# The attention stage's diagonal term and head maximum: added behind the turned sums, and spread by one product with repeated weights

## The chip, the cores and the metric

The kernel runs on one core of a Trainium2 chip, as one launch. The metric is the time of one execution on the device in microseconds (us), the median over several runs. The engines are TensorE (PE in the profile, its loads of stationary operands PEld), VectorE (DVE), ScalarE (ACT), GpSimd (POOL) and SyncE (SP).

## What is computed

A vision tower over 16 images of 512 tokens, width 192: Fourier features and a projection, attention with an optimal-transport plan in place of the usual scores, a layer norm, a mixture of eight experts (two per token), and a layer norm. The change lies in the attention alone. Cut to it (12 heads of width 16):

```python
def _sot(q):                                   # per image and head, N = 512
    qn = q / (norm(q, axis=-1) + 1e-08)
    C = where(eye, 1000.0, 1.0 - einsum('bhnd,bhmd->bhnm', qn, qn))
    log_K = -C / 0.1
    log_v = 0
    for _ in range(10):
        log_u = log_marg - logsumexp(log_K + log_v[..., None, :], axis=-1)
        log_v = log_marg - logsumexp(log_K + log_u[..., :, None], axis=-2)
    z = exp(log_u[..., :, None] + log_K + log_v[..., None, :])
    z = z / max(z, axis=(-2, -1))              # the head's own maximum
    return where(eye, 1.0, z)
attn = softmax(_sot(q) * 16 ** -0.5, axis=-1)
out = einsum('bhnm,bhmd->bhnd', attn, v)
```

## The kernel before, in words

Four stages follow one another: `embed` (features and first projection), `project` (q and v), `attend`, and `mix` with `combine` (experts and norms). Only `attend` is touched.

`attend` works on 48 groups of 4 heads (3 groups per image). The kernel matrix K of a head (512 x 512, four blocks of 128 rows, as high and low f16 part) is built once, and the 20 half iterations are products of K with a vector x, then a reciprocal. Three groups are in flight at any time. Phase G does four things side by side: it builds K of group G+1 (`build`), runs the first half iterations of group G (`young`), the later ones of group G-1 (`old`), and finishes group G-2 (`fin`, its last steps in phase G+1: `tail`). A phase has 10 cycles, `i = 5 * f + c`; f = 0 serves heads a = 0 and b = 1 of the group, f = 1 heads a = 2 and b = 3. The text calls a cycle c0 to c4 of either half. Phases 3 to 44 run in a hardware loop with one image (three phases) per turn; the others are written out.

In each cycle TensorE does `multiply(0)` and `multiply(1)`, each 64 narrow products (12 columns of weights, placed in one of four column strips of the array, L643). ScalarE copies the result out (`read_rows`, L771), TensorE turns it with two f32 products against constant weights each (`turn`, L653), and VectorE makes the next x from it with three small operations (`split`, L885 to L889), for which the next `multiply` waits.

What finishes a head h:

- `u_to_rows` (L677) brings u into rows; VectorE forms the plan z (`join` L908, `times_u` L920) and, block by block, the maximum of each row, and then of each partition (`head_max`, L925).
- Over the partitions the maximum goes by two products and two VectorE operations. `max_to_row` (L683) turns the column `head_max` into one row in PSUM; `largest` (L929) takes the maximum of this row on one partition (`all_max`, 1 x 1); `spread_max` (L687) multiplies it with a row of 4.0 on one partition (`fours`), so that every partition has 4 times the maximum; `scale_of` (L933) takes the reciprocal (`p_scale`). L683 stands in c2 (head a) and c4 (head b), behind the two `multiply` and ahead of `turn(0)`; L687 in the same cycle, ahead of `turn(1)`.
- ScalarE turns z into exp(z * p_scale - 0.25) (`weights`, L794).
- `times_v` (L697) multiplies with v: 16 f32 products of 17 columns of weights (16 of v and a one, for the row sum). Behind them stand 4 more (L700), which add v times the constant diagonal `lift` = 1 - exp(-0.25) for the tokens' own term. `times_v` stands in c4 (head a) and in c1 of the following half (head b).
- ScalarE copies the sums out (`read_v`, L798); `turn_v` (L707) turns them back with one f32 product of 128 columns of weights into `trp`; VectorE divides (`normalise`, L943, L947). `turn_v` stands in c0 and in c3.

Every engine works through its list strictly in the order in which it is written; semaphores join them (`after(engine, semaphore, count)` waits).

Of the kernel before, what the change touches and what calls it, by code (L numbers as in the profile page):

```python
# [488 lines left out]
def attend(nc, q_parts, v_parts, ident, pick_rows, att):  # L489
# [6 lines left out]
    with ExitStack() as ctx:  # L496
# [4 lines left out]
        def sem(name):  # L501
# [13 lines left out]
        fours = sb("fours", [1, P], F32)  # L515
# [12 lines left out]
        all_max = sb("all_max", [1, 1], F32)  # L528
# [13 lines left out]
        max_row, max_all = u_rows[0:1, 0:P], u_rows[:, P:P + 1]  # L542
# [13 lines left out]
        max_row_ready, all_max_ready, max_spread, scale_ready, p_ready = (  # L556
            sem("max_row_ready"), sem("all_max_ready"), sem("max_spread"), sem("scale_ready"), sem("p_ready"))
# [26 lines left out]
        def _(sp):  # L584
# [20 lines left out]
            def phase(G, t, s, young=False, old=False, build=False, fin=False, tail=False):  # L605
# [5 lines left out]
                if old:  # L611
                    after(sp, pv_ready, (G - 3) * GH)
                    load_v(t - 1 if s == 0 else t, (s + 2) % 3)
# [10 lines left out]
        def _(pe):  # L624
# [56 lines left out]
            def max_to_row(F, h):  # L681
                after(pe, head_max_ready, F * GH + h + 1)
                nc.tensor.matmul(max_row, head_max[:, :], eye[:, :], start=True, stop=True).then_inc(max_row_ready, 1)  # L683

            def spread_max(F, h):
                after(pe, all_max_ready, F * GH + h + 1)
                nc.tensor.matmul(max_all, fours[:, :], all_max[:, :], start=True, stop=True).then_inc(max_spread, 1)  # L687

            def times_v(F, s, h, image):
# [5 lines left out]
                for j in range(TB):  # L695
                    for c in range(TB):
                        nc.tensor.matmul(pv[32 * c:32 * c + HD + 1, 0:P], v_sb[s][:, j, h, :], plan[h % 2][:, j, c * P:(c + 1) * P],  # L697
                                         start=(j == 0), stop=False)
                for c in range(TB):
                    last = nc.tensor.matmul(pv[32 * c:32 * c + HD + 1, 0:P], v_sb[s][:, c, h, :], lift[:, :],  # L700
                                            start=False, stop=True)
                last.then_inc(pv_ready, 1)

            def turn_v(F, h):
                H = F * GH + h
                after(pe, pv_read, H + 1)
                nc.tensor.matmul(trp_flat, pv_sb[:, :], to_chunks, start=True, stop=True).then_inc(pv_turned, 1)  # L707

            def phase(G, t, s, young=False, old=False, build=False, fin=False, tail=False):
                mine, before, new = s, (s + 2) % 3, (s + 1) % 3  # L710
                t_fin, t_new = (t if s == 2 else t - 1), (t + 1 if s == 2 else t)
                for i in range(CYCLES):
# [13 lines left out]
                    if c == 2 and fin:  # L726
                        max_to_row(G - 2, a)
                    if c == 4 and fin:
                        max_to_row(G - 2, b)
# [4 lines left out]
                    if c == 0 and f == 0 and tail:  # L734
                        turn_v(G - 3, GH - 2)
                    if c == 0 and f == 1 and fin:
                        turn_v(G - 2, a - 2)
# [8 lines left out]
                    if c == 2 and fin:  # L746
                        spread_max(G - 2, a)
                    if c == 4 and fin:
# [1217 lines left out]
```

## Time and profile before

| | |
|---|---|
| time, median of 3 runs | 5770.17 us (5761.57 to 5798.24) |
| the profiled execution, its own time | 5812.22 us |
| its span in the trace | 5810.4 us |
| PE busy | 4788.6 us (82%) |
| DVE busy | 4015.8 us (69%) |
| ACT busy | 3119.7 us (54%) |
| POOL busy | 840.2 us (14%) |
| attention stage, from about 1582 to 4577 us | 2995 us; PE busy 2842.0, DVE 2146.6, ACT 1712.9 |

The profiled execution is one run, 42 us above the median of the runs. "Busy" of TensorE counts the modelled durations of single products, which overlap; how long it really takes for something is read from the starts of consecutive rows of the timeline.

### The profile page before, as it was taken

The page shows a single profiled execution, that of the slowest core. Times are in us where ns is not written, and L with a number is a line of the kernel's source. Part 1 is how long each engine was busy: PE and PEld are TensorE (multiplying, and loading weights), DVE is VectorE, ACT ScalarE, POOL GpSimd, SP SyncE. Part 2 cuts the span into 40 slices and gives each one's busy share as a digit, 9 for nine tenths or more (in the row PEclk, how much of TensorE's full clock was granted, in tenths as well). Part 3 has the DMA queues.
Part 4 walks back from the last instruction along what each step waited for, and adds up shares of the span by engine and source line. Part 5 has one row for each costly group of instructions (what it writes and reads, how often), then busy time and mean ns, then how long its engine had stood idle before and what let it go on. Part 6 is the DMA issues. An engine that isn't in the chain of part 4 may idle for free. (4 is left out here: it accounts for less than half of the span.)

```text
span 5810.4 us, 201644 instructions
## 1 busy us (share of the span) xinstructions
PE 4788.6 (82%) x86322; PEld 3667.1 (63%) x86323; DVE 4015.8 (69%) x8485; ACT 3119.7 (54%) x4426; POOL 840.2 (14%) x394
## 2 busy tenths in 40 slices
PE   4766776677679999999999999999999289699950
PEld 2444554454358888888888888887888245477740
DVE  8888888985537777777777777777777634355545
ACT  4665666664356556655556555565564223277740
POOL 2444444442000000000000000000000013400026
PEclk9888988888889999999999999999999656699985
DMA  1000000001310000000000000000000212222223
GB/s 55 24 24 24 13 24 24 24 13 42 101 26 15 15 20 15 17 18 15 20 15 19 16 15 20 15 19 16 15 16 7 83 54 75 88 64 69 68 64 98
DMA packets 186937, 198.44 MB, mean 34 GB/s; under 512 B 86848, under 2 KB 167040, under 8 KB 183552
## 3 DMA queue, kind: packets, MB, share of 16 engines
q1 hardware_dynamic: 173824, 160.79, 9.2%
q0 software_dynamic: 12288, 25.18, 1.4%
q8 instruction: 697, 11.42, 0.8%
q14 instruction: 128, 1.05, 0.1%
HBM read 123.00 MB, written 62.91 MB: 32 GB/s over the span
## 5 line engine op out<-in xcount | busy, mean ns | idle before, releaser
L643 PE MATMUL y_ps<-k_sb,x_sb 128*12 128x256 f16 x58368 | 1718.4, 276 | 30.1 <-issue 14.1
L643 PEld LDWEIGHTS y_ps<-k_sb,x_sb 128*12 128x12 bf16 x58368 | 1438.2, 89 | 227.9 <-issue 48.8
L257 PE MATMUL acc<-w_hl,feat_h 128*128 128x384 f16 x3456 | 645.1, 351 | 425.3 <-DVE h_sb L203 297.8
L771 ACT ACTIVATE y_sb<-y_ps 128x256 f32<-128x256 f32 x912 | 348.9, 383 | 1031.9 <-PE y_ps L643 1031.9
L257 PEld LDWEIGHTS acc<-w_hl,feat_h 128*128 128x128 f16 x3456 | 356.9, 104 | 688.7 <-issue 372.9
L150 POOL TENSOR_TENSOR feat_l<-work,feat_h 128x2048 f16<-128x2048 f32 x96 | 576.7, 6008 | 777.6 <-ACT feat_h L241 739.1
L780 ACT ACTIVATE k_new<-cos,k_bias 128x512 f32<-128x512 f32 x768 | 520.4, 682 | 162.9 <-PE cos L670 162.9
L653 PEld LDWEIGHTS turned_x<-rows_in,y_sb 128*128 128x128 f32 x3648 | 477.2, 191 | 138.4 <-issue 93.3
L653 PE MATMUL turned_x<-rows_in,y_sb 128*128 128x16 f32 x3648 | 552.5, 265 | 9.5 <-ACT y_sb L771 9.2
L920 DVE CUSTOM_DVE_ANT_0 plan<-plan,u_rows,v_last 128x512 f32<-128x512 f32 x768 | 535.3, 744 | 4.1
L885 DVE RECIPROCAL x_sb<-turned_x 128x16 f32<-128x16 f32 x864 | 223.6, 259 | 433.2 <-PE turned_x L653 433.1
L241 ACT ACTIVATE feat_h<-work 128x4096 f16<-128x4096 f32 x96 | 388.2, 4044 | 200.2 <-PE acc L264 198.2
L794 ACT ACTIVATE plan<-plan,p_bias,p_scale 128x1024 f32<-128x1024 f32 x384 | 464.3, 1238 | 11.8 <-DVE p_scale L933 11.8
L908 DVE TENSOR_TENSOR plan<-k_sb 128x1024 f32<-128x1024 f16 x384 | 459.8, 1218 | 0.0
L937 DVE TENSOR_TENSOR k_sb<-k_new,k_sb 128x2048 f16<-128x2048 f32 x192 | 436.7, 2274 | 30.1 <-ACT k_sb L788 30.1
L1112 POOL PARTITION_ALL_REDUCE all_maxes<-maxes x1 | 0.4, 374 | 3014.4 <-DVE maxes L1131 3014.4
L194 DVE TENSOR_TENSOR feat_l<-work,feat_h 128x2048 f16<-128x2048 f32 x96 | 320.2, 3335 | 155.5 <-ACT feat_h L241 155.5
L177 DVE TENSOR_SCALAR work<-xt,fr 128x2048 int32<-128x2048 f32 x144 | 387.9, 2720 | 0.0
L788 ACT ACTIVATE k_sb<-k_new 128x2048 f16<-128x2048 f32 x192 | 366.6, 1909 | 10.0
L235 ACT ACTIVATE work<-work 128x2048 f32<-128x2048 f32 x96 | 203.4, 2119 | 311.9 <-DVE work L186 309.6
L264 PE MATMUL acc<-w_hl,feat_l 128*128 128x192 f16 x3456 | 306.4, 248 | 34.2 <-DVE feat_l L194 31.0
L668 PE MATMUL cos<-q_right,q_left 128*128 128x512 f16 x768 | 259.5, 391 | 81.9 <-issue 37.9
(255 smaller groups left out, 7427.1 us busy)
## 6 DMA issues: line engine op xcount, KB each, us to landing
xt<-in_x_dram SPq DMA_DIRECT2D x16, 1280.0 KB, 5.8
x_in_sb<-expert_rows SPq DMA_DIRECT2D x39, 384.0 KB, 3.2
expert_results<-y_sb SPq DMA_DIRECT2D x39, 384.0 KB, 2.5
q_left<-q_parts SPq DMA_DIRECT2D x192, 64.0 KB, 2.9
q_right<-q_parts SPq DMA_DIRECT2D x192, 64.0 KB, 3.0
v_parts<-v_sb SPq DMA_DIRECT2D x16, 408.0 KB, 2.4
v_in_sb<-v_parts SPq DMA_DIRECT2D x48, 136.0 KB, 3.4
h_tokens<-h_sb SPq DMA_DIRECT2D x16, 384.0 KB, 2.5
```

The source lines that it names most:

```text
L150: nc.gpsimd.tensor_tensor(feat_l[n][:, 1, 0:hi], waves[n][:, 1, 0:hi], feat_h[n][:, 1, 0:hi], ALU.subtract).then_inc(low_cos_ready[n], 1)
L177: last = nc.vector.tensor_scalar(whole[:, lo:hi], xt[a][:, lo:hi], fr[:, f:f + 1], None, ALU.mult)
L241: nc.scalar.activation(feat_h[n][:, :, 0:hi], waves[n][:, :, 0:hi], ACT.Copy).then_inc(high_ready[n], 1)
L257: nc.tensor.matmul(acc[a][:, q, 0:2 * DIM], block_of, w_hl[:, k, :, :].rearrange("p a d -> p (a d)"), start=(k == 0), stop=False)
L643: last = nc.tensor.matmul(y[a][32 * c:32 * c + XW, :, :], high[:, j, XW * h:XW * (h + 1)], k_sb[s][:, h, :, at:at + P], start=(h == 0 and ...
L653: last = nc.tensor.matmul(tr_flat[a], y_sb[a][:, part, :], add_parts, start=(part == 0), stop=(part == 1))
L780: nc.scalar.activation(k_new[h % 2][:, c, :], cos[:, c % 2, :], ACT.Exp, bias=k_bias[:, 0:1], scale=1.0 / (REG * Q_SCALE ** 2), accum_out= ...
L788: nc.scalar.activation(k_sb[s][:, h, 0, :], k_new[h % 2][:, :, :].rearrange("p b n -> p (b n)"), ACT.Copy).then_inc(k_high, 1)
L794: nc.scalar.activation(part, part, ACT.Exp, bias=p_bias[:, 0:1], scale=p_scale[h % 2][:, 0:1]).then_inc(p_ready, 1)
L908: done = nc.vector.tensor_tensor(plan[h % 2][:, 2 * half:2 * half + 2, :].rearrange("p b n -> p (b n)"), k_sb[s][:, h, 0, cols], k_sb[s][: ...
L920: last = nc.vector.tensor_tensor_reduce(plan[h % 2][:, c, :], plan[h % 2][:, c, :], u_rows[:, :], v_last[s][:, c, h:h + 1], 0.0, ALU.mult, ...
L937: nc.vector.tensor_tensor(k_sb[s][:, h, 1, :], k_new[h % 2][:, :, :].rearrange("p b n -> p (b n)"), k_sb[s][:, h, 0, :], ALU.subtract).the ...
```

## The change

Two steps of the finish of a head are computed otherwise.

The diagonal: the four narrow f32 products at the end of `times_v` are gone. Instead `turn_v` first multiplies v, as the moving operand with 68 columns, by the diagonal `lift`, with 128 columns of weights, into `trp`, and the product that turns the sums is added to it.

The maximum: `max_to_row`, `largest` and `spread_max` are gone. `max_to_rows` uses the column `head_max`, repeated 128 times, as weights and a diagonal of 4.0 (`eye_four`) as moving operand, so that every partition gets the whole row of maxima (times 4). `scale_of` takes the maximum of its partition's row and then the reciprocal; both stand on VectorE ahead of `next_x(0)`. SyncE's wait before it loads v is now on `pv_turned`, since `turn_v` reads v.

```diff
@@ sync
                 if old:
-                    after(sp, pv_ready, (G - 3) * GH)
+                    after(sp, pv_turned, (G - 3) * GH)
                     load_v(t - 1 if s == 0 else t, (s + 2) % 3)
@@ tensor
-            def max_to_row(F, h):
+            def max_to_rows(F, h):
                 after(pe, head_max_ready, F * GH + h + 1)
-                nc.tensor.matmul(max_row, head_max[:, :], eye[:, :], start=True, stop=True).then_inc(max_row_ready, 1)
-
-            def spread_max(F, h):
-                after(pe, all_max_ready, F * GH + h + 1)
-                nc.tensor.matmul(max_all, fours[:, :], all_max[:, :], start=True, stop=True).then_inc(max_spread, 1)
+                nc.tensor.matmul(max_rows, head_max[:, :].to_broadcast([P, P]), eye_four[:, :], start=True,
+                                 stop=True).then_inc(max_rows_ready, 1)
@@ times_v
                 for j in range(TB):
                     for c in range(TB):
-                        nc.tensor.matmul(pv[32 * c:32 * c + HD + 1, 0:P], v_sb[s][:, j, h, :], plan[h % 2][:, j, c * P:(c + 1) * P],
-                                         start=(j == 0), stop=False)
-                for c in range(TB):
-                    last = nc.tensor.matmul(pv[32 * c:32 * c + HD + 1, 0:P], v_sb[s][:, c, h, :], lift[:, :],
-                                            start=False, stop=True)
+                        last = nc.tensor.matmul(pv[32 * c:32 * c + HD + 1, 0:P], v_sb[s][:, j, h, :],
+                                                plan[h % 2][:, j, c * P:(c + 1) * P], start=(j == 0), stop=(j == TB - 1))
                 last.then_inc(pv_ready, 1)
-            def turn_v(F, h):
+            def turn_v(F, s, h):
                 H = F * GH + h
                 after(pe, pv_read, H + 1)
-                nc.tensor.matmul(trp_flat, pv_sb[:, :], to_chunks, start=True, stop=True).then_inc(pv_turned, 1)
+                nc.tensor.matmul(trp, lift[:, :], v_sb[s][:, :, h, :], start=True, stop=False)
+                nc.tensor.matmul(trp_flat, pv_sb[:, :], to_chunks, start=False, stop=True).then_inc(pv_turned, 1)
@@ phase, tensor
-                    if c == 2 and fin:
-                        spread_max(G - 2, a)
-                    if c == 4 and fin:
-                        spread_max(G - 2, b)
@@ vector
-            def largest(F, h):
-                after(dve, max_row_ready, F * GH + h + 1)
-                nc.vector.tensor_reduce(all_max[:, :], max_row, AX_X, ALU.max).then_inc(all_max_ready, 1)
-
             def scale_of(F, h):
-                after(dve, max_spread, F * GH + h + 1)
-                nc.vector.reciprocal(p_scale[h % 2][:, :], max_all).then_inc(scale_ready, 1)
+                after(dve, max_rows_ready, F * GH + h + 1)
+                nc.vector.tensor_reduce(all_max[:, :], max_rows, AX_X, ALU.max).then_inc(all_max_ready, 1)
+                after(dve, all_max_ready, F * GH + h + 1)
+                nc.vector.reciprocal(p_scale[h % 2][:, :], all_max[:, :]).then_inc(scale_ready, 1)
```

How the order of instructions moves. On TensorE, at the end of a group's phase in the loop (c3 and c4 of f = 1), before; `pv` holds the sums with v, `u_rows` the maxima, `x2` that a row stands for two instructions:

```order
L653 MATMUL turned_x<-rows_in,y_sb 128x16 x2
L707 MATMUL pv<-rows_in,pv_sb 128x68
L643 MATMUL y_ps<-k_sb,x_sb 12x256 x128
L661 MATMUL cos<-eye_bf,x_sb 120x128 x2
L683 MATMUL u_rows<-eye,head_max 1x128
L653 MATMUL turned_x<-rows_in,y_sb 128x16 x2
L697 MATMUL pv<-plan,v_in_sb 17x128 x16
L700 MATMUL pv<-lift,v_in_sb 17x128 x4
L687 MATMUL u_rows<-all_max,fours 128x1
L653 MATMUL turned_x<-rows_in,y_sb 128x16 x2
```

And the same place with the change:

```order
L653 MATMUL turned_x<-rows_in,y_sb 128x16 x2
L701 MATMUL pv<-v_in_sb,lift 128x68
L702 MATMUL pv<-rows_in,pv_sb 128x68
L643 MATMUL y_ps<-k_sb,x_sb 12x256 x128
L661 MATMUL cos<-eye_bf,x_sb 120x128 x2
L683 MATMUL u_rows<-eye_four,head_max 128x128
L653 MATMUL turned_x<-rows_in,y_sb 128x16 x2
L694 MATMUL pv<-plan,v_in_sb 17x128 x16
L653 MATMUL turned_x<-rows_in,y_sb 128x16 x2
```

Five instructions behind L661 have gone (L700 four times, L687), one has come ahead of L643 (L701), and L683 has 128 columns of weights where it had one.

On VectorE in cycle c2 of the same phase, before, from the end of one `join` to the second `x`:

```order
L929 TENSOR_REDUCE all_max<-u_rows 1x1
L486 REGISTER_ALU
L885 RECIPROCAL x_sb<-turned_x 128x16
L486 ISA
L887 TENSOR_TENSOR x_sb<-x_sb 128x16
L486 REGISTER_ALU
L889 TENSOR_TENSOR x_sb<-x_sb 128x16
L933 RECIPROCAL p_scale<-u_rows 128x1
L486 REGISTER_ALU
L885 RECIPROCAL x_sb<-turned_x 128x16
```

With the change, from the reciprocal on (its line is now L922, that of `split` L876 to L880):

```order
L922 RECIPROCAL p_scale<-all_max 128x1
L486 REGISTER_ALU
L876 RECIPROCAL x_sb<-turned_x 128x16
L486 ISA
L878 TENSOR_TENSOR x_sb<-x_sb 128x16
L486 REGISTER_ALU
L880 TENSOR_TENSOR x_sb<-x_sb 128x16
L486 REGISTER_ALU
L876 RECIPROCAL x_sb<-turned_x 128x16
```

The reciprocal of the maximum has moved from behind the first x to ahead of it.

## Rows read from the trace of the kernel before

**Rows 1.** Windows, nine loop turns: length, busy of PE, PEld, DVE, ACT, POOL, clock.

```profile
1812.00:3441.00 1629.00, 1586.03 (x41228) 1323.82 (x41224) 1203.41 (x3405) 961.01 (x1838) 0.00 (x0) 0.98 0.07 17
```

**Rows 2.** Timeline of TensorE, c1 to c3, f = 1: start, us, instruction, count.

```profile
3024.90 0.40 PE L700 MATMUL pv<-lift,v_in_sb 128*17 128x128 f32 x8
3025.12 3.68 PE L643 MATMUL y_ps<-k_sb,x_sb 128*12 128x256 f16 x128
3028.61 0.38 PE L683 MATMUL u_rows<-eye,head_max 128*1 128x128 f32 x2
...
3029.88 0.22 PE L670 MATMUL cos<-eye_hide,eye_h 128*128 128x128 f16 x1
3030.02 0.38 PE L687 MATMUL u_rows<-all_max,fours 1*128 1x1 f32 x2
3030.33 0.62 PE L653 MATMUL turned_x<-rows_in,y_sb 128*128 128x16 f32 x4
3030.80 0.38 PE L677 MATMUL u_rows<-xt_sb,pick 128*128 128x128 bf16 x4
3031.11 3.67 PE L643 MATMUL y_ps<-k_sb,x_sb 128*12 128x256 f16 x128
3034.71 0.62 PE L653 MATMUL turned_x<-rows_in,y_sb 128*128 128x16 f32 x4
...
3035.66 0.22 PE L670 MATMUL cos<-eye_hide,eye_h 128*128 128x128 f16 x1
3035.72 0.57 PE L653 MATMUL turned_x<-rows_in,y_sb 128*128 128x16 f32 x4
3036.14 0.42 PE L707 MATMUL pv<-rows_in,pv_sb 128*128 128x68 f32 x2
```

**Rows 3.** Timeline of TensorE, end of c3 and c4, f = 0.

```profile
3006.49 3.67 PE L643 MATMUL y_ps<-k_sb,x_sb 128*12 128x256 f16 x128
3010.41 0.38 PE L683 MATMUL u_rows<-eye,head_max 128*1 128x128 f32 x2 [0.25 <-DVE head_max L925]
3010.72 0.62 PE L653 MATMUL turned_x<-rows_in,y_sb 128*128 128x16 f32 x4
3011.27 1.07 PE L697 MATMUL pv<-plan,v_in_sb 128*17 128x128 f32 x32
3012.15 0.40 PE L700 MATMUL pv<-lift,v_in_sb 128*17 128x128 f32 x8
3012.48 0.38 PE L687 MATMUL u_rows<-all_max,fours 1*128 1x1 f32 x2
```

**Rows 4.** Timeline of TensorE, c4, f = 1.

```profile
3040.09 0.33 PE L661 MATMUL cos<-eye_bf,x_sb 128*120 128x128 bf16 x2
3040.41 0.38 PE L683 MATMUL u_rows<-eye,head_max 128*1 128x128 f32 x2
```

**Rows 5.** Timeline of all engines, c0, f = 0.

```profile
2987.85 0.38 ACT L771 ACTIVATE y_sb<-y_ps 128x256 f32<-128x256 f32 x1 [2.97 <-PE y_ps L643]
...
2987.97 0.39 PE L707 MATMUL pv<-rows_in,pv_sb 128*128 128x68 f32 x2
...
2988.37 0.39 PE L653 MATMUL turned_x<-rows_in,y_sb 128*128 128x16 f32 x2
```

**Rows 6.** Timeline of VectorE, c4 of f = 0.

```profile
3010.20 0.16 DVE L925 TENSOR_REDUCE head_max<-row_max 128x1 f32<-128x4 f32 x1
```

**Rows 7.** Timeline of VectorE, c2 of f = 1.

```profile
3029.03 0.28 DVE L929 TENSOR_REDUCE all_max<-u_rows 1x1 f32<-1x128 f32 x1 [1.22 <-PE u_rows L683]
3029.58 0.26 DVE L885 RECIPROCAL x_sb<-turned_x 128x16 f32<-128x16 f32 x1 [0.27 <-PE turned_x L653]
```

**Rows 8.** Timeline of VectorE, last c4 of the stage.

```profile
4564.57 0.28 DVE L929 TENSOR_REDUCE all_max<-u_rows 1x1 f32<-1x128 f32 x1 [0.68 <-PE u_rows L683]
4567.21 0.17 DVE L933 RECIPROCAL p_scale<-u_rows 128x1 f32<-128x1 f32 x1 [2.37 <-PE u_rows L687]
```

**Rows 9.** Windows, behind a turn of the loop, columns as in rows 1.

```profile
3227.00:3233.50 6.50, 4.69 (x68) 2.54 (x68) 0.37 (x2) 0.00 (x0) 0.00 (x0) 0.50 0.03 8
```

More of the change, by code:

```diff
@@ L514, in attend @@
         k_bias, p_bias = sb("k_bias", [P, 1], F32), sb("p_bias", [P, 1], F32)
-        fours = sb("fours", [1, P], F32)
+        eye_four = sb("eye_four", [P, P], F32)
         q_left, q_right = three("q_left", [P, GH, TOKENS], F16), three("q_right", [P, GH, TOKENS], F16)
@@ L527, in attend @@
         row_max, head_max = sb("row_max", [P, TB], F32), sb("head_max", [P, 1], F32)
-        all_max = sb("all_max", [1, 1], F32)
+        all_max = sb("all_max", [P, 1], F32)
         p_scale = two("p_scale", [P, 1], F32)
@@ L541, in attend @@
         trp = trp_flat.rearrange("p (b d) -> p b d", b=TB)
-        max_row, max_all = u_rows[0:1, 0:P], u_rows[:, P:P + 1]
+        max_rows = u_rows[:, 0:P]
         XT = 2 * GH * XS
@@ L555, in attend @@
             sem("joined"), sem("u_rows_ready"), sem("plan_ready"), sem("head_max_ready"))
-        max_row_ready, all_max_ready, max_spread, scale_ready, p_ready = (
-            sem("max_row_ready"), sem("all_max_ready"), sem("max_spread"), sem("scale_ready"), sem("p_ready"))
+        max_rows_ready, all_max_ready, scale_ready, p_ready = (
+            sem("max_rows_ready"), sem("all_max_ready"), sem("scale_ready"), sem("p_ready"))
         pv_ready, pv_read, pv_turned, den_ready, att_ready = (
@@ L726, in phase @@
                     if c == 2 and fin:
-                        max_to_row(G - 2, a)
+                        max_to_rows(G - 2, a)
                     if c == 4 and fin:
-                        max_to_row(G - 2, b)
+                        max_to_rows(G - 2, b)
                     if young and i > 0:
@@ L734, in phase @@
                     if c == 0 and f == 0 and tail:
-                        turn_v(G - 3, GH - 2)
+                        turn_v(G - 3, mine, GH - 2)
                     if c == 0 and f == 1 and fin:
-                        turn_v(G - 2, a - 2)
+                        turn_v(G - 2, new, a - 2)
                     if c == 1 and build:
@@ L758, in phase @@
                     if c == 3 and f == 0 and tail:
-                        turn_v(G - 3, GH - 1)
+                        turn_v(G - 3, mine, GH - 1)
                     if c == 3 and f == 1 and fin:
-                        turn_v(G - 2, b - 2)
+                        turn_v(G - 2, new, b - 2)
             phases(pe, phase)
@@ L862, in _ @@
             nc.vector.memset(p_bias[:, :], -ATT_SCALE).then_inc(consts, 1)
-            nc.vector.memset(fours[:, :], 1.0 / ATT_SCALE).then_inc(consts, 1)
             dve.wait_ge(zeroed, START + 3)
@@ L877, in _ @@
             nc.vector.tensor_scalar(eye_hide[:, :], eye[:, :], HIDE, None, ALU.mult).then_inc(consts, 1)
+            nc.vector.tensor_scalar(eye_four[:, :], eye[:, :], 1.0 / ATT_SCALE, None, ALU.mult).then_inc(consts, 1)
             nc.vector.tensor_scalar(lift[:, :], eye[:, :], float(1.0 - np.exp(-ATT_SCALE)), None, ALU.mult).then_inc(consts, 1)
@@ L956, in phase @@
                     if c == 2 and fin:
-                        largest(G - 2, a)
-                    if c == 4 and fin:
-                        largest(G - 2, b)
-                    if young and i > 0:
-                        next_x(0, G * YOUNG + (i - 1), mine)
-                    if c == 2 and fin:
                         scale_of(G - 2, a)
@@ L965, in phase @@
                         scale_of(G - 2, b)
+                    if young and i > 0:
+                        next_x(0, G * YOUNG + (i - 1), mine)
                     if old:
```

## The prediction

> **What bounds the kernel now.** I read the windows first. In nine turns of the attention loop TensorE is busy 1586.0 of 1629 us, VectorE 1203.4, ScalarE 961.0 [rows 1]. So this stage should be as long as TensorE's list of instructions. Its busy time can't be used as a price, since narrow products overlap: 128 of them are shown as 3.67 us and the next row starts 3.60 later [rows 2]. A price is therefore the distance between the starts of two neighbouring rows. Then I looked for places where TensorE waits for others, as work added there is free and work removed there brings nothing. There is one in each group: in c4 of f = 0 the block of `multiply` ends 3.92 us after it began, where c2 has 3.49 for the same 128 products, and the row names VectorE's `head_max` [rows 2, 3]. Two f32 products stand as four records, so one f32 instruction is two records (halves).
>
> **The change, part by part.** All per group of four heads, in us.
>
> *A product's price.* `turn`, two f32 products with 128 columns of weights, takes 0.47 (3030.33 to 3030.80) or, behind another wide product, 0.42 (3035.72 to 3036.14) [rows 2]: 0.21 to 0.24 for one. A block of `multiply` takes 3.49 when a product with one column of weights follows (3025.12 to 3028.61), 3.60 when a wide one follows (3031.11 to 3034.71) [rows 2]. So going from narrow to wide weights costs 0.11.
>
> *c1, twice: the four diagonal products go.* L700 starts at 3024.90, the next block at 3025.12 [rows 2]: -0.22 each, **-0.44**.
>
> *c2, twice: the maximum.* The block before L683 now ends on a wide product: +0.11. L683 takes 0.31 to the next row now (3010.41 to 3010.72 [rows 3]), with one column of weights and 128 moving columns. Wide, it neither starts nor ends at a change of width; I take 0.24 as for `turn`: -0.07. L687 is gone, 0.31 (3030.02 to 3030.33), and the way to it, 0.14 (3029.88 to 3030.02), shrinks to the 0.06 of 3035.66 to 3035.72; `turn(1)` behind it goes from 0.47 to 0.42 [rows 2]. Sum 0.11 - 0.07 - 0.31 - 0.08 - 0.05 = -0.40 each, **-0.80**.
>
> The trace has no product with repeated weights 128 wide and 128 f32 columns moving. Its bounds are 0.21, a half `turn`, and 0.62, if all that L683 (many moving columns) and L687 (wide weights) take now added up. I take 0.24: it is nearest to `turn` in weights, and nothing in the trace says that repeating a column costs. The Trainium skill speaks against the wide form: in "TensorE: Matmul & The Clock Gate", section "LDWEIGHTS (loading the stationary operand)", a load takes its number of columns divided by 1.2 in ns, so 128 columns in two halves would be 0.21 where one column is next to nothing. If that came on top of today's 0.31 in each of 180 products, the sum below would be some 50 smaller; the trace's `turn`, at 0.21 to 0.24 for such a load together with its product, says that it doesn't come on top. "TensorEngine Tiling (Array Packing)", section "Key Properties", says that a change of tiling mode drains the engine; the 0.11 and the shorter way to a wide product behind a wide one agree, and by that rule L687 (one partition) costs two drains that now go.
>
> *c4, f = 1.* L683 follows the bf16 pair L661, 0.32 (3040.09 to 3040.41 [rows 4]), at a change of width that goes: -0.11. L683 itself -0.07. L700 goes, 0.33 (3012.15 to 3012.48 [rows 3]), but the way from narrow to wide stays, 0.11: -0.22. L687 goes: -0.31. Sum **-0.71**.
>
> *c4, f = 0.* With a wide L683 the block would take 3.60, against 3.92 now: 0.32 is waiting. That wait runs from `turn(1)` of c3, from which VectorE's x, plan and maximum follow, so the lift product that c3 now gets (0.24) vanishes in it, and L683 starts when it did. After it -0.07 - 0.22 - 0.31: **-0.60**.
>
> *The lift product elsewhere.* c3 of f = 1 and c0 of f = 1, 0.24 each: **+0.48**. In c0 of f = 0 TensorE waits for ScalarE's copy (2987.85 + 0.38 = 2988.23): L707 to L653 is 0.40 (2987.97 to 2988.37), 0.16 over a product's 0.24 [rows 5]; **+0.08**. If such covers were complete everywhere, the 0.56 would all be free; if none existed, c0 and c3 of f = 0 would add 0.4.
>
> *VectorE.* The row maximum is now taken on 128 partitions instead of one. L929 takes 0.28 for 128 columns on one, the maximum over 4 columns on 128 partitions 0.16 [rows 6, 7]; the price lies between 0.28 and, if columns and partitions both counted in full, 0.44; I take 0.28. The reciprocal (0.17 [rows 8]) moves ahead of the x that `multiply(0)` waits for. In c2, counted from L683's start: L929 starts at 0.42 (3028.61 to 3029.03), ends at 0.70, the reciprocal at some 0.92 with a small handover. L885 starts 0.66 after its `turn` (3028.92 to 3029.58; 3028.92 is L683 plus 0.31) [rows 2, 7], which is at 0.24 + 0.66 = 0.90. So x starts at 0.92, earlier than today's 0.97, and three steps of at most 0.26 end by 1.70. `multiply(0)` comes at 2.50 before (3028.61 to 3031.11) and at about 2.0 with the change (2.50 - 0.07 - 0.31 - 0.08 - 0.05). Slack 0.3; nothing waits, also at 0.44. Without that cover each 0.1 over it costs 0.2 a group. SyncE's new wait is on a `turn_v` of the phase before, and stands behind waits on that phase's c3: nothing.
>
> *Sum.* -0.44 - 0.80 - 0.71 - 0.60 + 0.48 + 0.08 = -1.99 a group. Phases 2 to 46 are built alike: 45 x 1.99 = 90. The last three phases are chains through all engines. In the last c4 `all_max` is ready at 4564.85 and `p_scale` begins at 4567.21, since L687 stands behind `times_v` [rows 8]; now it would begin at once: 2.3. For the dozen heads of these phases I estimate 8 (from 2.3, this one alone, to 14, all six c4). Together **-98**. Against the profiled execution, 5812.2, this gives 5714; that run lies 42 above the median of the runs, and I take the difference from the median: 5770 - 98 = **5672**.
>
> **The rivals.**
>
> *The wide maximum is dear* (0.62 instead of 0.24, four a group, 1.52 of the 1.99 lost): 45 x 0.47 + 8 = 29, so 5741. For it: no row shows such a product. Against it: every wide f32 product shown costs 0.21 to 0.24. 0.15.
>
> *Hidden anyway*: VectorE's chain to `head_max`, already waited for once a group [rows 3], takes over and holds the length of a group: 5770. Against it: that wait is 0.32 of some 60 us (1629 by 27 groups [rows 1]), and the added product moves TensorE later there, not earlier; VectorE idles 1.22 ahead of L929 in c2 [rows 7]. 0.04.
>
> *The clock.* Behind a turn of the loop the granted clock is 0.50, the 1.2 GHz level, for 6.5 us at least [rows 9], in the loop 0.98 in the mean [rows 1]; half of that time, 3.3, is lost at each of 13 turns. The change moves how much TensorE did before and after a turn. If low stretches doubled: +43, 5715, 0.05. If they vanished: -43, 5629, 0.07.
>
> *Slower.* The load of 128 times the same column could be served one by one from the same place and take far longer. It stands in line in TensorE 192 times; the gain is gone from 98 / 180 = 0.54 more, that is 0.78 for the product, and from 0.86 more (1.1 in all) the kernel is over 1% slower. At 1.3 it would be 180 x 1.06 - 98 = +93, 5863. Nothing in the trace shows a price like that. 0.03.
>
> **How the numbers follow.** My forecast, with the bounds of its small terms, covers 5640 to 5705: 0.66. The range reaches into the dear maximum and a vanished low clock: 5630 to 5725, leaving out some 0.18. About 1%, 58 us, is what a measurement can tell from no change. Faster by more than that (below 5712): forecast, vanished clock, half of the doubled one and a little of the dear maximum, 0.79. Within 1%: 0.18. Slower: 0.03.
>
> **What would show it.** PE's rows: c2 from the start of a block to the start of the next 5.99 before (3025.12 to 3031.11), 5.6 after; L683 to the next row 0.24; the narrow block of `times_v` followed by the next row without L700; the wait on `head_max` in c4 of f = 0 down to about 0.1; a turn of the loop some 6 shorter. VectorE: `p_scale` directly behind `all_max`. I am wrong if L683 takes 0.4 or more, if `multiply(0)` waits for an x, or if a group is shorter by less than 1.3.

## The result

The changed kernel takes 5633.86 us (median of 4 runs, 5627.77 to 5638.48) where the kernel before, measured with it, takes 5765.87. The ratio is 0.9756, with a 95% interval from 0.9729 to 0.9783: 2.4% faster, 125 to 156 us of 5770. The forecast was 98, and the medians lie 132 apart. The direction and the mechanism held; the forecast size was too small by a quarter. In us the time lies just inside the range, whose edge is 5630; as a share of the kernel before, that edge is 0.9757 of 5770 and the measured ratio 0.9756, just outside. One execution of a kernel below, the first of the maximum alone, took 15304 us at a granted clock of 0.37; neither its time nor its trace is used.

The span of the profiled execution fell from 5810.4 to 5626.0, by 184. That is more than the runs show, and the difference doesn't lie in attention. The last product of the attention stage, before and after:

```profile
4572.57 0.70 PE L707 MATMUL pv<-rows_in,pv_sb 128*128 128x68 f32 x2 [0.40 <-ACT pv_sb L798]
```

```profile
4447.68 0.63 PE L702 MATMUL pv<-rows_in,pv_sb 128*128 128x68 f32 x2
```

From there to the end it is 1238 before and 1178 after, in code that the change doesn't touch. A second trace of the kernel before (below) has 1183 there, so that most of these 60 us belong to the single execution. Attention itself, from its first L661 (the one product pair that stands once in each phase) to its last product, went from 1726.64 to 4572.57 (2845.9) to 1729.89 to 4447.68 (2717.8): 128 less, about what the medians show.

The timeline of TensorE in the changed kernel, first c0 to c2 of f = 0, which answers to [rows 2] and [rows 5]:

```profile
2884.98 0.39 PE L701 MATMUL pv<-v_in_sb,lift 128*128 128x68 f32 x2
2885.21 0.39 PE L702 MATMUL pv<-rows_in,pv_sb 128*128 128x68 f32 x2
2885.43 0.57 PE L653 MATMUL turned_x<-rows_in,y_sb 128*128 128x16 f32 x4
...
2891.04 1.07 PE L694 MATMUL pv<-plan,v_in_sb 128*17 128x128 f32 x32
2891.92 3.68 PE L643 MATMUL y_ps<-k_sb,x_sb 128*12 128x256 f16 x128
2895.53 0.49 PE L683 MATMUL u_rows<-eye_four,head_max 128*128 128x128 f32 x2
2895.85 0.52 PE L653 MATMUL turned_x<-rows_in,y_sb 128*128 128x16 f32 x4
2896.22 0.38 PE L668 MATMUL cos<-q_right,q_left 128*128 128x512 f16 x1
...
2897.18 0.38 PE L677 MATMUL u_rows<-xt_sb,pick 128*128 128x128 bf16 x4
2897.49 3.67 PE L643 MATMUL y_ps<-k_sb,x_sb 128*12 128x256 f16 x128
```

and c3 and c4 of f = 0, which answers to [rows 3]:

```profile
2902.52 0.42 PE L701 MATMUL pv<-v_in_sb,lift 128*128 128x68 f32 x2
2902.77 0.39 PE L702 MATMUL pv<-rows_in,pv_sb 128*128 128x68 f32 x2
2903.09 3.67 PE L643 MATMUL y_ps<-k_sb,x_sb 128*12 128x256 f16 x128
2906.79 0.49 PE L683 MATMUL u_rows<-eye_four,head_max 128*128 128x128 f32 x2
2907.11 0.52 PE L653 MATMUL turned_x<-rows_in,y_sb 128*128 128x16 f32 x4
2907.56 1.07 PE L694 MATMUL pv<-plan,v_in_sb 128*17 128x128 f32 x32
2908.56 0.62 PE L653 MATMUL turned_x<-rows_in,y_sb 128*128 128x16 f32 x4
```

and c4 of f = 1, which answers to [rows 4]:

```profile
2879.91 0.33 PE L661 MATMUL cos<-eye_bf,x_sb 128*120 128x128 bf16 x2
2880.07 0.44 PE L683 MATMUL u_rows<-eye_four,head_max 128*128 128x128 f32 x2
2880.35 0.52 PE L653 MATMUL turned_x<-rows_in,y_sb 128*128 128x16 f32 x4
2880.80 1.07 PE L694 MATMUL pv<-plan,v_in_sb 128*17 128x128 f32 x32
2881.79 0.62 PE L653 MATMUL turned_x<-rows_in,y_sb 128*128 128x16 f32 x4
```

Again the distances of starts are read. In c2, from one block of `multiply` to the next, it was 5.99 [rows 2] and is 5.57 (2891.92 to 2897.49). The wide L683 takes 0.32, and `turn` behind it 0.37. VectorE in that cycle, to be held against [rows 7]:

```profile
2925.01 0.29 DVE L920 TENSOR_REDUCE all_max<-u_rows 128x1 f32<-128x128 f32 x1 [1.33 <-PE u_rows L683]
2925.34 0.16 DVE L922 RECIPROCAL p_scale<-all_max 128x1 f32<-128x1 f32 x1
2925.44 0.26 DVE L876 RECIPROCAL x_sb<-turned_x 128x16 f32<-128x16 f32 x1
```

The maximum on 128 partitions takes 0.29, as on one (0.28), and the next x begins 0.95 behind L683 (2924.49), against 0.97 before.

What TensorE waited for, in nine turns of the loop, from the view of waits (engine, line, what it waited for: us in total, times, longest). The kernel before, its products and one line of its loads of weights (PEld):

```profile
PE cos L668 <- issue: 25.2, 9, 3.2
PE y_ps L643 <- issue: 9.5, 10, 1.3
PE u_rows L683 <- DVE head_max L925: 6.9, 27, 0.3
PEld y_ps L643 <- DVE x_sb L889: 1.8, 9, 0.2
```

The changed kernel, its products:

```profile
PE cos L668 <- issue: 25.9, 9, 3.2
PE y_ps L643 <- issue: 6.4, 12, 1.0
```

No product waits for another engine in this view any more, and the loads no longer wait for an x. A little is left of the wait on `head_max`: in c4 of f = 0 the block takes 3.70 (2903.09 to 2906.79) where 3.60 is its length ahead of a wide product, so 0.1, as forecast. What else is left is "issue": waits that no semaphore explains, a long one at each turn of the loop (L668 is the first product of the body), and a shorter one in `multiply` soon behind it. The second kind became important, as the runs show.

### The profile page after: what moved, and what is told of

The parts are those of the page before. It is cut to its first block and busy times, and to the rows that moved or that the text cites. A ratio compares the mean times of both kernels' runs of the same rounds, so it can differ in the third digit from the quotient of the medians.

```text
span 5626.0 us, 198571 instructions
## 1 busy us (share of the span) xinstructions
PE 4651.3 (83%) x84786; PEld 3606.0 (64%) x84787; DVE 4007.4 (71%) x8485; ACT 3109.6 (55%) x4426; POOL 837.1 (15%) x394
## 5 line engine op out<-in xcount | busy, mean ns | idle before, releaser
L643 PE MATMUL y_ps<-k_sb,x_sb 128*12 128x256 f16 x58368 | 1705.6, 275 | 21.5 <-DVE x_sb L880 13.0
L643 PEld LDWEIGHTS y_ps<-k_sb,x_sb 128*12 128x12 bf16 x58368 | 1433.4, 88 | 209.9 <-issue 38.7
L653 PEld LDWEIGHTS turned_x<-rows_in,y_sb 128*128 128x128 f32 x3648 | 478.1, 191 | 118.9 <-issue 71.6
L653 PE MATMUL turned_x<-rows_in,y_sb 128*128 128x16 f32 x3648 | 527.0, 258 | 8.6 <-ACT y_sb L762 8.4
L876 DVE RECIPROCAL x_sb<-turned_x 128x16 f32<-128x16 f32 x864 | 223.3, 258 | 367.2 <-PE turned_x L653 366.8
L785 ACT ACTIVATE plan<-plan,p_bias,p_scale 128x1024 f32<-128x1024 f32 x384 | 464.3, 1238 | 9.7 <-DVE p_scale L922 9.7
L264 PEld LDWEIGHTS acc<-w_hl,feat_l 128*128 128x128 f16 x3456 | 293.4, 99 | 53.2 <-DVE feat_l L194 37.0
```

The lines of the kernel that those rows point to most:

```text
L264: last = nc.tensor.matmul(acc[a][:, q, 0:DIM], block_of, w_hl[:, k, 0, :], start=False, stop=(k == NCH - 1))
L643: last = nc.tensor.matmul(y[a][32 * c:32 * c + XW, :, :], high[:, j, XW * h:XW * (h + 1)], k_sb[s][:, h, :, at:at + P], start=(h == 0 and ...
L653: last = nc.tensor.matmul(tr_flat[a], y_sb[a][:, part, :], add_parts, start=(part == 0), stop=(part == 1))
L785: nc.scalar.activation(part, part, ACT.Exp, bias=p_bias[:, 0:1], scale=p_scale[h % 2][:, 0:1]).then_inc(p_ready, 1)
```

## The experiments

Two lengths are read from each trace, from the distances of the L661 rows: a plain group (median of 29 in and around the loop that hold no turn), and how much a group with a turn is longer than that (mean over the 13 turns). With them, the number of TensorE's instructions from the first product behind a turn to its second stop: products, loads of weights and the few instructions on registers, each counted. The expectations call these 25, 81 and so on "products"; that was the wrong word, 25 are 12 products, 12 loads and one on registers:

| kernel | median us | ratio to before | plain group | extra of a turn | second stop behind |
|---|---|---|---|---|---|
| before | 5766 | 1 | 58.0 and 58.2 by turns | 7.2 | 25, at all 13 |
| before, second trace | 5794 | 0.9987 (0.9962 to 1.0012) | 58.2 | 8.6 | 25, at all 13 |
| changed | 5634 | 0.9756 (0.9729 to 0.9783) | 55.7 | 5.7 | 81 at 5 of 13 |
| changed again | 5631 | 0.9753 (0.9714 to 0.9793) | 55.7 | 5.5 | 81 at 4 |
| diagonal alone | 5760 | 0.9940 (0.9912 to 0.9967) | 57.7 | 4.3 | 65 at 4 |
| maximum alone, second run | 5700 | 0.9822 (0.9790 to 0.9854) | 56.4 | 7.7 | 41, at all 13 |
| spread over 128 partitions | 5791 | 0.9977 (0.9957 to 0.9997) | 57.5 | 7.6 | 25, at all 13 |
| lift product twice | 5707 | 0.9842 (0.9810 to 0.9874) | 56.5 | 5.5 | 73 at 4 |
| before, code moved | 5776 | 1.0002 (0.9972 to 1.0032) | 58.4 | 5.8 | none at 25; 338 at 5 |
| changed, code moved | 5657 | 0.9797 (0.9757 to 0.9836) | 55.7 | 6.9 | 25, at all 13 |
| times_v first in c4 | 5630 | 0.9749 (0.9702 to 0.9796) | 55.8 | 4.5 | 81 at 3 |
| times_v first, f = 0 alone | 5627 | 0.9693 (0.9665 to 0.9721) | 55.4 | 5.8 | 81 at 3 |
| the same, code moved | 5625 | 0.9690 (0.9660 to 0.9719) | 55.4 | 5.1 | none |

A stop is a distance of 0.6 us or more between the starts of two neighbouring products. Ratios are each to runs of the kernel before on the same chip; its median was 5799, 5783 and 5803 on the three occasions of the experiments, so only ratios are compared across them.

**The two parts alone.** The diagonal, on the kernel before:

```diff
                 for j in range(TB):
                     for c in range(TB):
-                        nc.tensor.matmul(... plan ..., start=(j == 0), stop=False)
-                for c in range(TB):
-                    last = nc.tensor.matmul(... lift ..., start=False, stop=True)
+                        last = nc.tensor.matmul(... plan ..., start=(j == 0), stop=(j == TB - 1))
...
+                nc.tensor.matmul(trp, lift[:, :], v_sb[s][:, :, h, :], start=True, stop=False)
-                nc.tensor.matmul(trp_flat, pv_sb[:, :], to_chunks, start=True, stop=True).then_inc(pv_turned, 1)
+                nc.tensor.matmul(trp_flat, pv_sb[:, :], to_chunks, start=False, stop=True).then_inc(pv_turned, 1)
```

> Only the diagonal part of the change, on the kernel before. Theory A (a group is as long as TensorE's list, priced by the distances of rows): the narrow block of times_v goes in c1 and c4, 0.22 each, four in all, -0.88; the lift product costs 0.22 in c3 and c0 of f = 1, and nothing in c3 of f = 0 (wait on head_max, 0.43 now) and c0 of f = 0 (wait on ScalarE's copy). A group goes from 58.1 to 57.65, the kernel 20 us faster, about 5746. Rival B (lift is paid at all four places): 58.1, no change. Rival C (the diagonal carries most of the 132 us that were measured): 60 us or more faster.

Measured: ratio 0.9940, 19 to 51 us of 5799 by the interval, 35 in the middle. A plain group lost only 0.3, less than the 0.44 expected, which is 13 us over 45 groups; but a turn of the loop costs 4.3 over it instead of 7.2, 38 over 13 turns in this trace. The greater part of what this part brought, by this trace, was in a place of which no theory had spoken. B and C are out. The 0.3 is not the rows' price either: the plain groups took 57.5, 57.7 or 58.0, and they differ in one block of `multiply`, the same in each group, which took its 3.60 in the groups of 57.5 and up to 4.4 in the others. The undisturbed group is thus 0.5 shorter than 58.0; what stops TensorE in that block is taken up below.

The maximum alone is the changed kernel with the lines above put back. It was run twice, and the trace is that of the second run.

> Only the maximum part, on the kernel before. Theory A: a group takes 55.73 + 0.44 = 56.2, the kernel is about 110 us faster (5655) if the shorter cost of the loop's turns (extra over a plain group 6.6 before, 5.6 with the change) belongs to this part, about 95 (5670) if it doesn't. Rival B (the two parts help each other, neither reaches its share): less than 80 us.

> Only the maximum part, once more, for its trace. By the place of the code: its loop begins 16 instructions earlier than that of before (4 of TensorE's instructions less for each of the 4 heads ahead of the loop), so the second stop should stand 41 products behind every turn, with a turn dear as before, about 7 over a plain group; a plain group 55.7 + 0.3 = 56.0 (0.3 is what the diagonal alone gained). Rival (the shorter turns came with the removed products of the maximum): a turn at 5 to 6 over a plain group.

Measured, first and second: 0.9861 (0.9823 to 0.9899) and 0.9822 (0.9790 to 0.9854). A plain group 56.4, 1.7 less than before; a turn 7.7 over it, as dear as before. The middle values of the two parts, 0.6% and 1.4 or 1.8%, add up to 2.0 or 2.4%, the whole being 2.4%: no sign that they help or hinder each other. The second stop stood where it was expected, 41 instructions behind each turn: 4 products of the cosines and 16 of the block, as many loads, and one on registers:

```profile
2847.48 0.61 PE L668 MATMUL cos<-q_right,q_left 128*128 128x512 f16 x1 [3.88 <-issue]
...
2848.66 1.03 PE L643 MATMUL y_ps<-k_sb,x_sb 128*12 128x256 f16 x16
2850.20 2.23 PE L643 MATMUL y_ps<-k_sb,x_sb 128*12 128x256 f16 x48 [0.51 <-issue]
```

**What made L687 dear.**

```diff
-        fours = sb("fours", [1, P], F32)
+        fours = sb("fours", [P, P], F32)
...
-        all_max = sb("all_max", [1, 1], F32)
+        all_max = sb("all_max", [P, 1], F32)
...
-                nc.vector.tensor_reduce(all_max[:, :], max_row, AX_X, ALU.max).then_inc(all_max_ready, 1)
+                nc.vector.tensor_reduce(all_max[0:1, :], max_row, AX_X, ALU.max).then_inc(all_max_ready, 1)
```

> The kernel before, with L687 contracting over 128 partitions (fours has 128 rows, all_max is zero on all partitions but the first; same result). Theory A (L687 was dear because it used one partition, so that TensorE had to change its shape before and behind it): the way from L670 to it falls from 0.15 to 0.06, from it to turn from 0.31 to 0.21 to 0.24, the turn behind it from 0.47 to 0.42 or less; a group 0.6 to 0.8 shorter, the kernel some 30 us faster. Rival B (any f32 product costs that between two others): rows and group as before, within 5 us.

Measured, in c2:

```profile
3077.47 0.22 PE L670 MATMUL cos<-eye_hide,eye_h 128*128 128x128 f16 x1
3077.53 0.33 PE L687 MATMUL u_rows<-all_max,fours 128*128 128x1 f32 x2
3077.72 0.60 PE L653 MATMUL turned_x<-rows_in,y_sb 128*128 128x16 f32 x4
3078.22 0.38 PE L677 MATMUL u_rows<-xt_sb,pick 128*128 128x128 bf16 x4
```

From L670 it is 0.06 (before 0.14), to `turn` 0.19 (before 0.31): a product over all partitions, with 128 times the rows, costs 0.20 less with the way to it. `turn` behind it took 0.50, not the 0.42 expected, where it was 0.47 before, so that 0.17 is left of it. A plain group fell to 57.5, 0.6 less for four such products, as A says. In the time it is 0.2% (0.03 to 0.43%), 8 us, where the group promises 28; the turns were 0.4 dearer each, 5 us of it, and the rest is not located. So of the 0.45 that L687 and the way to it cost in c2, 0.17 came from its one partition and not from the product. "TensorEngine Tiling (Array Packing)" of the Trainium skill, section "Key Properties", says that changing the tiling mode drains the engine. If a product over one partition counts as another mode, which no run here shows, this trace agrees, and 0.17 is the price of the way there and back.

**The price of a wide f32 product.**

```diff
+                nc.tensor.matmul(trp, lift[:, :], v_sb[s][:, :, h, :], start=True, stop=True)
                 nc.tensor.matmul(trp, lift[:, :], v_sb[s][:, :, h, :], start=True, stop=False)
```

> The changed kernel with the lift product issued twice (the second overwrites the first; same result). Measures a wide f32 product. Theory A: the rows from the first lift to the next grow by 0.22, a group by 0.22 in c3 and c0 of f = 1, 0.2 in c0 of f = 0 and 0.12 in c3 of f = 0 (a wait of 0.10 takes the rest): 56.5 instead of 55.73, the kernel about 35 us slower than the changed one (5669), still faster than before. Rival B (loads of constant weights vanish beside the product ahead): under 0.1 each, no difference to the changed kernel.

```profile
2900.37 0.39 PE L701 MATMUL pv<-v_in_sb,lift 128*128 128x68 f32 x2
2900.60 0.39 PE L702 MATMUL pv<-v_in_sb,lift 128*128 128x68 f32 x2
2900.82 0.39 PE L703 MATMUL pv<-rows_in,pv_sb 128*128 128x68 f32 x2
2901.05 0.57 PE L653 MATMUL turned_x<-rows_in,y_sb 128*128 128x16 f32 x4
```

0.23, 0.22, 0.23: that is what one costs, with 68 moving columns as with 16. The rule for loads that the prediction weighed (the Trainium skill, "TensorE: Matmul & The Clock Gate", section "LDWEIGHTS (loading the stationary operand)") gives 0.21 for two loads of 128 columns; the trace agrees, and with up to 68 moving columns the product itself adds next to nothing. A plain group went to 56.5, 0.8 more for four of them, so that all four were paid but for the 0.1 of a wait. Ratio 0.9842 against 0.9756: some 50 us, with an uncertainty of about 25, and 36 of it by the groups.

**Is it the place of the loop's code?** The kernel before, behind one turn of its loop:

```profile
3228.69 0.60 PE L643 MATMUL y_ps<-k_sb,x_sb 128*12 128x256 f16 x8
3230.59 3.16 PE L643 MATMUL y_ps<-k_sb,x_sb 128*12 128x256 f16 x56 [1.29 <-issue]
```

In this kernel the second stop stands behind exactly 25 instructions at every turn (4 products of the cosines and 8 of the block, as many loads, and one on registers), with the change behind 81, with the diagonal alone behind 65; where there is another, it stands 257 further on (338). Smaller stops keep the same places. In the loops of the 13 traces, 242 neighbouring products of one block of `multiply` start more than 0.25 us apart, where 0.03 is usual and 0.06 at the low clock; every one of them stands at the place of the second stop, or a multiple of 256 of TensorE's instructions behind it, to within 2. Those in the plain groups of the diagonal alone stand there too. That looks like code that is brought in pieces of one size, with the turn landing at some place in its piece; what brings it isn't in the trace. The diff moves this place, since each head worked off ahead of the loop now takes fewer instructions. To test it without touching the loop, idle products are put ahead of the first phase:

```diff
+            for _ in range(100):
+                nc.tensor.matmul(u_rows[:, 0:P], eye_bf[:, :], eye_bf[:, :], start=True, stop=True)
             phases(pe, phase)
```

100 in the kernel before, 28 in the changed one, two instructions each.

> The changed kernel with 28 idle bf16 products (56 instructions, 2 us) ahead of the first phase: its loop then begins where that of before does. Theory A (place of the code): the second stop stands 25 products behind every turn, 1.2 us or more, a turn costs about 7 over a plain group instead of 5.7; the kernel is 13 x 1.5 + 2, some 20 us slower than the changed one. Rival B (removed work): a turn costs 5.7, 2 us slower.

```profile
2827.83 0.61 PE L668 MATMUL cos<-q_right,q_left 128*128 128x512 f16 x1 [2.71 <-issue]
...
2829.01 0.60 PE L643 MATMUL y_ps<-k_sb,x_sb 128*12 128x256 f16 x8
2830.95 3.16 PE L643 MATMUL y_ps<-k_sb,x_sb 128*12 128x256 f16 x56 [1.33 <-issue]
2834.04 0.55 PE L677 MATMUL u_rows<-xt_sb,pick 128*128 128x128 bf16 x4
```

The stop came back at all 13 turns, behind the same eight products of the block as in the kernel before, and the block's rest then ran at a granted clock of 0.50, the 1.2 GHz level. A turn costs 6.9 over a plain group, the kernel is 26 us slower than the changed one beside it (5656.8 against 5630.9; all four runs of it are slower than all four of the other), with a loop that is word for word the same. By the L661 rows 18 of the 26 lie at the turns, and the idle products take some 2 (an estimate). A, not B. The same kernel unmoved:

> The changed kernel once more, on the chip of the three runs beside it, so that they are compared with it under one clock. Both theories: a group 55.7, ratio to the kernel before about 0.976.

Its turn, where no second stop falls, from the first trace of the changed kernel:

```profile
2824.51 0.60 PE L668 MATMUL cos<-q_right,q_left 128*128 128x512 f16 x1 [2.67 <-issue]
...
2825.68 2.87 PE L643 MATMUL y_ps<-k_sb,x_sb 128*12 128x256 f16 x64
2828.49 0.40 PE L677 MATMUL u_rows<-xt_sb,pick 128*128 128x128 bf16 x4
```

From the block's start to L677 it is 2.8 here and 5.0 in the moved kernel; at a granted clock of 1.00 64 products take 1.85 (2882.90 to 2884.75 in the changed kernel).

> The kernel before, with 100 idle bf16 products (200 instructions of TensorE with their loads, about 6 us in all) ahead of the first phase, so that the loop's code lies elsewhere; the loop itself is word for word that of before. In the trace of before TensorE stops a second time, for 1.2 to 1.7 us, 25 products behind each turn of the loop; with the change 81 products behind it, or not at all; such stops lie 256 products apart. Theory A (the second stop and the long low clock come from where the loop's code begins, not from the work that was removed): the second stop stands 81 products behind the turn and is rarer, the low clock shrinks, a turn costs 5 to 6 over a plain group instead of 7.2; the kernel is 13 x 1.5 = 20 less 6, some 14 us faster than before. Rival B (removed work does it): stops and low clock as before, the kernel 6 us slower.

Here the stop at 25 is gone at all turns (it stands at 338, at 5 of them), and a turn costs 5.8 instead of 7.2 or 8.6. But the time didn't fall: 1.0002. The first stop at a turn grew (3.7 in the mean instead of 3.2), and short stops of 0.8 now stand inside plain groups, which went from 58.0 and 58.2 to between 57.9 and 59.1. So the place of the code decides the second stop in both directions, and moving it is no sure gain: what one stop gives, other stops in the body can take.

The low clock goes with the second stop. In the group with a turn the granted clock stood at 0.50 for 7.9 and 11.1 us in the mean in the two traces of the kernel before, for 7.9, 8.4 and 6.8 in the three others that have the second stop at every turn (maximum alone, spread over 128 partitions, changed with the code moved), and for 3.7 to 5.5 in the eight that have not.

**The kernel before, a second trace.**

> The kernel before once more, for a second trace of it. If the 60 us by which its last stage was longer than that of the changed kernel (1238 against 1178) belong to single executions, it shows another value here, near 1180 to 1220; if they belong to the kernel, 1238 again. Attention 2804 from the first to the last product of L661 in both cases.

Its last product of attention starts at 4603.71, with a span of 5787.0: 1183 for the last stage. The 60 us were the execution's. Attention took longer there, 2824 between the first and last L661 rows instead of 2804, with a turn at 8.6. Two traces of one kernel can thus differ by 20 us in attention, by 1.4 us at each turn, and by 55 in the last stage.

**Can the order give more?** TensorE goes from narrow to wide weights and back in each c4: `multiply`, then L683 and `turn`, then the narrow `times_v`, then `turn`. Put directly behind `multiply`, `times_v` saves one pair:

```diff
                     if old:
                         multiply(1, G, before, i)
+                    if c == 4 and fin:
+                        times_v(G - 2, new, a, t_fin)
+                    if old:
                         if i == CYCLES - 1:
                             turn_x(G, before, build)
...
-                    if c == 4 and fin:
-                        times_v(G - 2, new, a, t_fin)
```

> The changed kernel with times_v of head a directly behind the two multiply in c4, ahead of the maximum and of turn(0); the same instructions. Theory A (each way from narrow to wide weights and back costs, and one pair of them goes; the wait on head_max in c4 of f = 0 is covered too): c4 shrinks by 0.25 to 0.4, a group from 55.7 to about 55.1, the kernel 27 us faster than the changed one. Rival B (turn(0) and its x come 0.9 later and multiply(0) of the next cycle waits for them, which eats it): group 55.7 or more, a wait of PE on DVE x_sb in the rows.

A plain group stayed at 55.8, though c4 shrank. What it gave came back one cycle and a half later as a wait:

```profile
1906.31 0.57 PE L653 MATMUL turned_x<-rows_in,y_sb 128*128 128x16 f32 x4
1907.42 3.67 PE L643 MATMUL y_ps<-k_sb,x_sb 128*12 128x256 f16 x128 [0.55 <-DVE x_sb L881]
```

B was right that a wait for an x eats the gain, but named the wrong one. It is the first x of the new group, which VectorE makes last in f = 1:

```profile
1904.46 2.29 DVE L927 TENSOR_TENSOR k_sb<-k_new,k_sb 128x2048 f16<-128x2048 f32 x1 [0.64 <-ACT k_sb L780]
1906.67 0.25 DVE L877 RECIPROCAL x_sb<-row_sums 128x16 f32<-128x16 f32 x1
```

It stands behind the low part of K (2.29), and that waits for ScalarE's high part, which begins when the block of `multiply` is read. This chain doesn't hang on c4's products at all. It is the next bound of a group. In c4 of f = 0 there is no new group, so the order was changed there alone:

> The changed kernel with times_v directly behind multiply in c4 of f = 0 alone. Theory A (the narrow-to-wide ways saved and the covered wait are real, 0.33 a group; in c4 of f = 1 they were given back, since the chain ScalarE high part, VectorE low part, first x did not move): a group at 55.4, no wait on first x, 45 x 0.33 = 15 us faster than the changed kernel. Rival B (the chain to first x, or another, holds the group anyway): 55.7.

A plain group 55.4, the 0.33 expected. The ratio is 0.9693, against 0.9756 and 0.9753 of the changed kernel on other chips; they were not timed side by side, so that 15 us by the groups is shown (2677 to 2662 from the first to the last L661) and the rest of the difference is open. With the code moved by 44 products more (88 instructions):

> The same with 44 idle bf16 products ahead of the first phase, so that 249 instead of 81 products lie between the turn of the loop and the next place where TensorE can stop. Theory A (the place of the code sets the second stop): stops, if any, 249 products behind a turn, a turn costs 4.5 or less over a plain group; against the one above 13 x 1 - 2.5, some 10 us faster. Rival B: a turn costs the same 5.5 and the kernel is 2.5 slower.

No second stop at any turn, and a turn at 5.1 instead of 5.8, where 4.5 or less was expected. From the first to the last L661 it is 2652 instead of 2662; the times, 5625.2 and 5626.5, can't tell it from nothing, so the 10 us expected are not shown.

## Where the prediction held, and where it was short

**Mechanism.** That a group is as long as TensorE's list, and that prices are distances between rows, held: the parts alone, the doubled product and the changed order all moved the group by about what the rows said, but for the diagonal alone (0.3 in the median for 0.44, with stops in one block) and the one case in which a wait took over. The wide maximum costs 0.32, not 0.62, VectorE's reduction 0.29, and no x came late. Of the rivals only the one on the clock came in, and in part: the low clock in the group with a turn shrank from 7.9 us to 4.5 and did not vanish. The forecast fell short by two steps of its sum: the prices of the wide products in a group, 17 us, and the turns of the loop, put at nothing, 19 us or more. Both follow.

**The sum, term by term**, per group:

| term | forecast | measured | read from |
|---|---|---|---|
| c1, twice, L700 gone | -0.44 | -0.44 | block 0.88 behind L694 (2891.04 to 2891.92) |
| c2, twice | -0.80 | -0.84 | 5.99 to 5.57 |
| c4, f = 1, from L661 to `turn(1)` | -0.71 | -0.82 | 0.32 + 2.07 + 0.31 [rows 4, 3] to 1.88 (2879.91 to 2881.79) |
| c3 and c4, f = 0 | -0.60 | -0.61 | lift +0.22; block to `turn(1)` 6.30 [rows 3] to 5.47 |
| lift in c3 and c0, f = 1 | +0.48 | +0.44 | e.g. 2884.98 to 2885.21, and the doubled product |
| lift in c0, f = 0 | +0.08 | 0.0 | L701 to L653 0.45 instead of 0.40, `turn` shorter |
| group | -1.99 | -2.27; by L661 rows -2.36 | |

The group of before that the rows are from is 58.01 long, from this row to that of [rows 4]:

```profile
2982.08 0.33 PE L661 MATMUL cos<-eye_bf,x_sb 128*120 128x128 bf16 x2
```

In the changed kernel it is 55.74 (2879.91 to 2935.65), so that the terms account for all of it. The 0.09 up to 2.36 is in the mean: the other plain group of each turn was 58.2 before, since a load for `multiply` waited 0.2 for VectorE's x there (the PEld line above, nine times in nine turns). This wait, which the change removed, the prediction didn't know; it had spoken of one wait in a group.

The mis-sized step of a group is the pricing of the wide products by a single row each, and the forecast fell short by 0.37. Of it, 0.11 is in c4 of f = 1. There the sum took 0.11 off the way from L661 and 0.07 off "L683 itself", 0.18. In fact L661, L683 and the `turn` behind them, all three wide now, went from 0.32 + 0.31 + 0.55 to 0.16 + 0.28 + 0.45, 0.29 less. Another 0.12 is the lift product, which was taken at 0.24 and costs 0.22, and nothing in c0 of f = 0. Then 0.09 is the wait for x, 0.04 c2, 0.01 the rest. In c2 two errors nearly met: L683 was taken as cheaper (0.24) than it is (0.32), but `turn` behind it was left at 0.47, and behind a wide product it takes 0.37. 45 groups of 0.37 are 17 us of the missing 34 (by the medians) to 43 (by the ratio).

**The turns of the loop** are the step that the sum didn't have: it put their change at nothing. The rival on the clock spoke of 3.3 lost at each turn, which might vanish or double, and laid it to how much TensorE does around a turn. The stop and the low clock behind it go together, and the runs tie both to another thing. A turn cost 7.2 over a plain group and costs 5.7, 1.5 less at 13 turns, 19 us; and what changed is where, among places 256 instructions apart, the loop's body begins. That follows from how many instructions stand ahead of it, and can be read from the trace of before in one place: the wait of 1.29 us put down to "issue" in the block behind each turn, which the prediction didn't name or price. That the place decides was shown on the changed kernel, where moving it back costs 26 us, and half shown on the kernel before, where the stop left but the time stayed.

**The last three phases** gave 6, not 8: 54.80 to 52.73, 45.22 to 42.85 by the L661 rows, and 1.5 behind the last. In the last c4 `p_scale` begins 0.03 behind `all_max`, as expected; of the 2.3 that this gave, the whole stretch kept 1.5. What took the rest was not followed.

```profile
4440.43 0.29 DVE L920 TENSOR_REDUCE all_max<-u_rows 128x1 f32<-128x128 f32 x1 [0.89 <-PE u_rows L683]
4440.75 0.16 DVE L922 RECIPROCAL p_scale<-all_max 128x1 f32<-128x1 f32 x1
```

Together: 45 x 2.36 + 19 + 6 = 131, where attention shows 128 and the medians 132. The forecast's 98 plus 17 plus 19 less 2 is the same number. That it fits so closely is partly luck. By the second traces of both kernels a turn went from 8.6 to 5.5, which is 40 us at 13 turns and not 19, and attention was 151 shorter from the first to the last L661, not 127. The term of the turns is thus known only as 19 to 40; the interval of the runs, 125 to 156, holds the sum with either.

**The base.** The advice to take the difference from the median and not from the profiled execution was sound: that execution was 42 us slow, and its last stage was 55 longer than in the second trace.

## What to carry to other kernels

Price a product on a busy TensorE by the distance to the next row, and both neighbours with it: the same f32 product costs 0.19 or 0.31 by whether it keeps to all 128 partitions or takes one, and the one behind it 0.37 or 0.47. Look for "issue" waits at a fixed number of instructions behind each turn of a loop: here they depend on where its code begins, so an edit ahead of it can bring or take time (26 us in one kernel here, nothing in the other), which is then no merit of the edit. And before an engine's list is shortened once more, look for the chain that doesn't hang on it.

## What the runs showed of the hardware that I had not expected

- TensorE stops at places in its instruction stream that lie 256 of its instructions apart (257 from the first to the second), if it comes to them soon behind a jump: behind 25 instructions at 13 of 13 turns (distances of 1.2 to 2.1 us), behind 41 at 13 of 13 (0.9 to 1.9), behind 65 at 4, behind 73 at 4, behind 81 at 3 to 5, behind 249 at none. The first stop, at the jump itself, is 2.8 to 4.0 us in the mean of each trace; what sets it was not tried.
- A product over one partition is dearer with its surroundings than one over 128, by 0.17 us in c2.
- Weights that repeat one column 128 times load like others: a load record of L683 takes 0.19, as one of `turn`. From L683 to the next row it is 0.28 to 0.32 with 128 moving f32 columns, against 0.22 to 0.23 for a product with 68.
